# Grouped convolution by three products per image pair in place of four

## The reference, cut to what matters

```python
# x (32, 64, 1024), cond (32, 128), weight (64, 16, 9), c_weight (64, 128), bias (64,), kernel (1024, 1024) bool
out = lax.conv_general_dilated(x, weight, window_strides=(1,), padding=[(4, 4)],
                               dimension_numbers=('NCH', 'OIH', 'NCH'), feature_group_count=4)
ctx = jnp.einsum('nd,od->no', cond, c_weight)
out = out + ctx[:, :, None] + bias[None, :, None]
w = kernel * 2.0 - 1.0
y = scale * jnp.einsum('bsi,if->bsf', out, w)
return x + y
```

## Time and profile before

| | us |
|---|---|
| three runs | 180.5, 180.7, 181.5; median 180.7 |
| profiled execution | 180.59 |
| its span | 178.8 |
| TensorE busy | 171.2 (96%) |
| VectorE busy | 127.5 (71%) |
| ScalarE busy | 68.1 (38%) |
| GpSimd busy | 7.4 (4%) |
| granted TensorE clock, mean | 0.99 of full |

### The profile page before, as it was taken

One profiled execution on the slowest core, in us unless ns is written; L12 is line 12 of the kernel. 1 busy time (PEld: TensorE's weight loads), 2 busy tenths in 40 slices (PEclk: granted clock), 3 DMA queues, 4 the chain that ended last, 5 costly groups with the idle time before them and its releaser, 6 DMA issues.

```text
span 178.8 us, 2874 instructions
## 1 busy us (share of the span) xinstructions
PE 171.2 (96%) x1010; PEld 147.5 (83%) x1010; DVE 127.5 (71%) x188; ACT 68.1 (38%) x77; POOL 7.4 (4%) x18
## 2 busy tenths in 40 slices
PE   7699999999999999999999999999999999998991
PEld 2379888898989889988989898988998898986781
DVE  5736466979996877687675967596766877587662
ACT  3203993566452543329071634237061502042000
POOL 4230600000000000000000000000000000000000
PEclk9969999999999999999999999999999999999999
DMA  5589697768886792776757793778463650005006
GB/s 216 132 152 279 206 262 188 186 105 207 192 283 164 104 343 47 109 167 125 283 84 175 116 318 56 130 146 204 192 96 55 90 233 0 2 0 235 4 0 235
DMA packets 23629, 27.35 MB, mean 153 GB/s; under 512 B 2752, under 2 KB 19072, under 8 KB 23616
## 3 DMA queue, kind: packets, MB, share of 16 engines
q1 hardware_dynamic: 22176, 25.63, 56.8%
q0 software_dynamic: 368, 1.07, 2.4%
q10 hardware_dynamic: 1072, 0.48, 1.3%
HBM read 10.32 MB, written 8.40 MB: 105 GB/s over the span
## 4 chain that ended last, share of the span: by engine, by line
PE 93%; DMA 2%; DVE 1%; ACTq 1%; issue 0%; DVEq 0%
PE ps_conv L658 33%; PE ps_A L681 28%; PE ps_C L681 14%; PE ps_B L681 7%; DMA taps_nat<-weight 2%; PE ps_B L698 2%; PE ps_A L698 2%; PE ps_toep L698 2%; PE ps_C L698 2%; PE ps_toep L681 1%; PE ps_toep L636 1%; PE ps_C L647 1%; DVE sums L214 1%; PE ps_A L624 1%; DVE x_nat L513 0%
## 5 line engine op out<-in xcount | busy, mean ns | idle before, releaser
L658 PEld LDWEIGHTS ps_conv<-toeplitz,x_blk 128*128 128x128 f32 x512 | 60.4, 194 | 2.6 <-issue 0.8
L658 PE MATMUL ps_conv<-toeplitz,x_blk 128*128 128x128 f32 x512 | 60.8, 278 | 0.0
L475 DVE TENSOR_TENSOR y_sum<-ps_conv,shift 128x512 f32<-128x512 f32 (+1 forms) x33 | 22.2, 674 | 17.4 <-PE ps_conv L658 12.4
L373 ACT CAST hi_S<-sums 128x512 fp32r<-128x512 f32 x28 | 16.6, 620 | 43.4 <-DVE sums L492 42.7
L373 ACT CAST hi_A<-y_sum 128x512 fp32r<-128x512 f32 x24 | 14.0, 616 | 41.5 <-DVE y_sum L475 41.5
L358 ACT COPY x_phase<-x_nat 128x1032 f32<-128x1032 f32 x13 | 28.3, 2177 | 3.0 <-DMA x_nat<-x 3.0
L513 DVE SCALAR_TENSOR_TENSOR x_nat<-ps_A,scale_col,x_nat 128x512 f32<-128x512 f32 x27 | 20.3, 750 | 11.2 <-PE ps_A L681 11.2
L502 DVE TENSOR_TENSOR lo_S<-sums,hi_S 128x512 fp32r<-128x512 f32 x28 | 19.0, 680 | 0.0
L502 DVE TENSOR_TENSOR lo_A<-y_sum,hi_A 128x512 fp32r<-128x512 f32 x24 | 16.3, 682 | 1.7 <-ACT hi_A L373 1.7
L681 PE MATMUL ps_A<-sign_T,hi_S 128*128 128x512 f32 x56 | 16.2, 412 | 1.1 <-DVE x_nat L513 0.9
L681 PE MATMUL ps_A<-sign_T,lo_S 128*128 128x512 f32 x56 | 15.0, 389 | 0.0
(11 more groups left out here) (104 smaller groups left out, 174.3 us busy)
## 6 DMA issues: line engine op xcount, KB each, us to landing
x_nat<-x SPq DMA_DIRECT2D x16, 512.0 KB, 4.2
out<-x_nat SPq DMA_DIRECT2D x15, 512.0 KB, 4.8
x_blk<-x_phase SPq DMA_DIRECT2D x118, 64.5 KB, 2.5
w_bytes<-w_bool SPq DMA_DIRECT2D x2, 512.0 KB, 6.3
shift<-shift_dram POOLq DMA_DIRECT2D x1, 768.0 KB, 6.1
x_blk<-x_phase ACTq DMA_DIRECT2D x6, 64.5 KB, 3.7
x_blk<-x_phase POOLq DMA_DIRECT2D x4, 64.5 KB, 3.0
out<-x_nat SPq DMA_DIRECT2D x1, 256.0 KB, 2.9
```

Source lines behind the costliest of these rows:

```text
L373: nc.scalar.copy(hi[k][:, :, :], flat(operand(k))).then_inc(hi_ok[k], 1)
L475: nc.vector.tensor_tensor(y_sum[r][:, u, a, :].rearrange("m u a o -> m a u o"), ps_conv[:, a, u, :], shift_of(d, r, a).unsqueeze(2).to_bro ...
L658: now = nc.tensor.matmul(ps_conv[:, a].rearrange("m u o -> m (u o)"), x_blk[r][:, a, s:s + M], toeplitz[:, s, g].rearrange("r u o -> r u ( ...
```

## The change

*Three products.* Let the output rows m be even or odd. With x phases e = 0, 1, 2 (columns 2k, 2k+1, 2k+2), T0 and T1 the two halves of the Toeplitz form, the even output is x0 T0 + x1 T1 and the odd output x1 T0 + x2 T1. The changed kernel computes M1 = (x0 - x1) T0, M2 = x1 (T0 + T1) and M3 = (x1 - x2) T1; even = M1 + M2, odd = M2 - M3. x_phase holds the three in turn at a step of three floats (K = 64 columns each): GpSimd writes the two differences by one subtraction with 1024 results (differences), ScalarE copies the odd phases, 512 (odd_phases). Both images of the pair give one weight load of 128 columns at a step of 12 bytes, so one pair has 3 x 4 matmuls of 128 columns, in three banks of ps_conv, that of the middle product first. Blocks are 192 columns a phase in place of 129. Double 0 keeps four products; its phase copies have 1536 columns in place of 1032.

*Shift.* In doubles 1 to 7 one fp32r matmul of 512 columns over 64 rows puts the shift into the middle bank, from its high and low parts (shift_parts) and a 0/1 matrix (of_image) that GpSimd makes in two copies of 2048 columns on 32 rows each. The way through DRAM goes. The early matmul has 256 columns in place of 512.

*From banks to y.* ScalarE copies the middle bank (middle), VectorE adds and subtracts (y_of), giving y_two with (image, k) on the partitions. Four DMAs a pair of 128 KB each, issued by ScalarE (to_parity), carry it to y_sum with (parity, k) on the partitions. The rows of w_bool are loaded in that order too, by four DMAs in place of two.

*Parts and order.* High and low parts are made for two operands at once: A (A11 and A12), S12, S34, and A22 alone. S1 to S4 move from the end of step d - 1 to the start of step d. The convolution of pair (1, 0) follows plain product 5 in place of 4. x_nat keeps 11 pairs in place of 16, and a load waits for the store of the pair that it overwrites.

```diff
-EARLY = 8
+EARLY = 4
-CONV_AFTER = {4: 0, 6: 1}
+CONV_AFTER = {5: 0, 6: 1}
 ...
             def to_blocks(d, r):
-                sp.wait_ge(conv_done[r], 2 * d)
-                sp.wait_ge(phase_ok[r], B * (d + 1))
-                for a in range(NG):
-                    to_block(sp, r, a, blk_in[r][a // GROUPS])
+                if d == 1:
+                    sp.wait_ge(conv_0[r], 2)
+                else:
+                    for m in range(3):
+                        sp.wait_ge(m_done[m], order(d - 1, r) + 1)
+                sp.wait_ge(dif_ok[r], d)
+                sp.wait_ge(odd_ok[r], d)
+                for g in range(GROUPS):
+                    for i in range(2):
+                        a = i * GROUPS + g
+                        sp.dma_start(x_blk[r][:, 2 * g + i], x_phase[r][a * CG:(a + 1) * CG]).then_inc(blk_in[r], 16)
 ...
+            def differences(d, r):            # GpSimd
+                x_wait(pool, d, r)
+                first = line(d, r, 0, PAD + L + PAD)
+                left, right = (bass.AP(first.tensor, first[:, c:c + 1].offset, [first.ap[0], [1, B], [B, 2], [2 * B, K]])
+                               for c in (0, B))
+                nc.gpsimd.tensor_tensor(x_phase[r][:, :, :].rearrange("r q (k e) -> r q e k", e=3)[:, :, 0::2], left, right, ALU.subtract).then_inc(dif_ok[r], 1)
 ...
+            def odd_phases(d, r):             # ScalarE
+                x_wait(act, d, r)
+                nc.scalar.copy(x_phase[r][:, :, 1::3], line(d, r, B, B + L).rearrange("r (k p q) -> r q k p", p=2, q=B)[:, :, :, 0]
+                               ).then_inc(odd_ok[r], 1)
+            def middle(d, r):
+                act.wait_ge(m_done[1], order(d, r) + 1)
+                if d > 1:
+                    act.wait_ge(y_in[r], 16 * 4 * (d - 1))
+                nc.scalar.copy(y_two[r][:, 1].rearrange("m u (g o) -> m g u o", g=GROUPS), ps_conv[:, 1]).then_inc(mid_ok, 1)
+            def to_parity(d, r):
 ...
+                for p, made in ((0, y_even_ok), (1, y_odd_ok)):
+                    act.wait_ge(made, order(d, r) + 1)
+                    for i in range(2):
+                        act.dma_start(y_sum[r][p * K:(p + 1) * K, i], y_two[r][i * K:(i + 1) * K, p]).then_inc(y_in[r], 16)
 ...
             def step(d):                      # ScalarE
-                for k in ("S3", "S4", "A22"):
-                    high_part(k, d)
                 if runs(d, 4):
-                    to_phases(d + 2, 0)
+                    odd_phases(d + 2, 0)
+                high_part("S12", d)
                 if runs(d, 2):
-                    high_part("A12", d + 1)
-                    high_part("A11", d + 1)
+                    middle(d + 1, 0)
+                high_part("S34", d)
+                high_part("A22", d)
+                if runs(d, 2):
+                    to_parity(d + 1, 0)
+                    middle(d + 1, 1)
                 if runs(d, 4):
-                    to_phases(d + 2, 1)
+                    odd_phases(d + 2, 1)
                 if runs(d, 2):
-                    high_part("S1", d + 1)
-                    high_part("S2", d + 1)
+                    high_part("A", d + 1)
+                    to_parity(d + 1, 1)
             def first_double():
 ...
+                high_0("A11")
+                odd_phases(1, 0)
+                act.wait_ge(w_in[1], 32)
                 sign("B11", 1)
-                to_phases(1, 1)
+                odd_phases(1, 1)
                 sign("B12", 1)
+                high_0("A21")
+                middle(1, 0)
+                odd_phases(2, 0)
+                middle(1, 1)
+                to_parity(1, 0)
+                odd_phases(2, 1)
+                high_part("A", 1)
+                to_parity(1, 1)
 ...
+            def y_of(d, r):                   # VectorE
+                n = order(d, r)
+                even, uneven = (y_two[r][:, p].rearrange("m u (g o) -> m g u o", g=GROUPS) for p in range(2))
+                dve.wait_ge(mid_ok, n + 1)
+                dve.wait_ge(m_done[0], n + 1)
+                if d > 1:
+                    dve.wait_ge(y_in[r], 16 * 4 * (d - 1))
+                nc.vector.tensor_tensor(even, ps_conv[:, 0], uneven, ALU.add).then_inc(y_even_ok, 1)
+                dve.wait_ge(m_done[2], n + 1)
+                nc.vector.tensor_tensor(uneven, uneven, ps_conv[:, 2], ALU.subtract).then_inc(y_odd_ok, 1)
 ...
             def step(d):                      # VectorE, as it stands after
+                if d > 1:
+                    sum_up("C21_A", d - 1)
+                combine("S1", d)
+                combine("S2", d)
+                sum_up("C11_P2", d)
+                combine("S3", d)
+                combine("S4", d)
+                sum_up("C11_P1", d)
+                low_part("S12", d)
+                if runs(d, 2):
+                    y_of(d + 1, 0)
+                sum_up("C12_A", d)
+                low_part("S34", d)
+                sum_up("C22_C", d)
+                low_part("A22", d)
+                if runs(d, 2):
+                    y_of(d + 1, 1)
+                sum_up("C22_A", d)
+                if last(d):
+                    finish_last(d)
+                else:
+                    low_part("A", d + 1)
+                    sum_up("C12_C", d)
 ...
             def conv(d, r):                   # TensorE
+                n = order(d, r)
 ...
+                pe.wait_ge(blk_in[r], 16 * NG * d)
+                for m, taps, read in ((1, 2, mid_ok), (0, 0, y_even_ok), (2, 1, y_odd_ok)):
+                    if n:
+                        pe.wait_ge(read, n)
+                    if m == 1:
 ...
+                        nc.tensor.matmul(ps_conv[:, m], of_image[:, first:first + 2].rearrange("n i k -> n (i k)"),
+                                         shift_parts[:, :].rearrange("n (g o) -> n g o", g=GROUPS).unsqueeze(2)
+                                         .to_broadcast([2 * N, GROUPS, B, CG]), start=True, stop=False, skip_group_check=True)
                     for g in range(GROUPS):
+                        now = nc.tensor.matmul(ps_conv[:, m, g].rearrange("m u o -> m (u o)"),
+                                               x_blk[r][:, 2 * g:2 * g + 2].rearrange("r b n -> r (b n)")[:, m::3],
+                                               toeplitz[:, taps, g].rearrange("r u o -> r (u o)"), start=m != 1, stop=True,
+                                               skip_group_check=True)
+                    now.then_inc(m_done[m], 1)
```

More of the change, by code:

```diff
@@ L76, with conv_product_kernel @@
                 "C21_A": "P4"}
-def conv_product_kernel(nc, x, cond, bias, weight, c_weight, w_bool, scale, shift_dram, out):
+def conv_product_kernel(nc, x, cond, bias, weight, c_weight, w_bool, scale, out):
     x_pairs = x.rearrange("(j a) c l -> j (a c) l", a=2)
@@ L224, in signs_in, with group, parts, images @@
             rows = slice(half * KH, (half + 1) * KH)
-            eng.dma_start(w_bytes[:, rows, :], w_bool.rearrange("(m p) f -> m p f", p=B)[:, rows, :]).then_inc(w_in[half], 16)
+            for p in range(2):
+                eng.dma_start(w_bytes[p * K:(p + 1) * K, rows, :],
+                              w_bool.rearrange("(k p u) f -> p k u f", p=2, u=B)[p][:, rows, :]).then_inc(w_in[half], 16)
         def operand(k):
+            if k in s_sum:
+                return s_sum[k]
             half = slice(0, KH) if k in ("A11", "A21") else slice(KH, B)
-            return s_sum[k][:, :, :, :] if k in s_sum else y_sum[int(k[1]) - 1][:, half, :, :]
-        def flat(ap):
-            return ap.rearrange("m u a o -> m u (a o)")
+            return y_sum[int(k[1]) - 1][:, :, half, :].rearrange("m i u c -> m u i c")
+        def group(k):
+            if k == "A":
+                return y_sum[0][:, :, :, :].rearrange("m i u c -> m u i c")
+            if k in ("S12", "S34"):
+                n = 0 if k == "S12" else 2
+                return sums[:, n:n + 2].rearrange("m n u i c -> m (n u i c)")
+            return operand(k)
+        def parts(of, k):
+            n = OPERANDS.index(SPLITS[k][0])
+            both = of[:, n:n + len(SPLITS[k])]
+            if k in ("S12", "S34"):
+                return both.rearrange("m n u c -> m (n u c)")
+            return both.rearrange("m n u (i c) -> m (n u) i c", i=2)
+        def images(ap):
+            return ap.rearrange("m u (i c) -> m u i c", i=2)
         @block.sync
@@ L361, in high_part, with high_0 @@
+            def high_0(k):
+                act.wait_ge(y_0, 3 if k == "A12" else 4 * int(k[1]))
+                nc.scalar.copy(images(hi[k]), operand(k)).then_inc(hi_0[k], 1)
             def high_part(k, d):
-                if k in s_sum:
-                    act.wait_ge(s_ok[k], d)
-                elif d == 0 and k == "A12":
-                    act.wait_ge(y_ok, 3)
+                if k in ("S12", "S34"):
+                    for part in SPLITS[k]:
+                        act.wait_ge(s_ok[part], d)
@@ L367, in high_part @@
                 else:
```

(14 more changed lines are left out.)

366 lines of the change are left out of this document (182 added, 184 removed).

## The result

| | before | after |
|---|---|---|
| median of the runs, us | 180.99 (4 runs) | 224.76 (222.7 to 226.3, 4 runs) |
| span of the profiled execution | 178.8 | 223.0 |
| ratio | | 1.238 (95%: 1.228 to 1.248) |

Forecast was 178.8 us in a range of 175.0 to 188.5. The kernel became 24% slower. The medians are of all runs; ratios and, from here on, differences between two kernels leave out a run that took over 1.5% longer than the fastest of its kernel (224.3 us for after). The page of after has rows that answer to the earlier trace rows: the new convolution, its weight loads, and GpSimd with VectorE. Columns: busy us, mean ns of one, then the engine's idle time before them and its releaser.

A forecast was written before the change was run, and what follows sets the result against it. TensorE's own work was taken as the bound: 178.8 span + 5.3 for the first double - 7.0 for 11 later convolutions + 0.2 in the last step = 177.3, 179.1 with the 1.8; stated as 178.8, range 175.0 to 188.5.

The forecast's parts named there:

- TensorE's records: Convolution matmuls with weights at a 12-byte step: 0.109 us a record taken, 24 records in 2.61 us.
- the forecast's largest gain: Convolutions from the second double on: 2.84 us a pair against 3.48, 0.64 less, 9.0 us over 14 pairs.
- nothing waits for them: GpSimd's two subtractions a step, 3.6 us taken for each (2.2 to 4.4), claimed to delay nothing in the steady stretch.
- The lock: Rival: VectorE operations with two SBUF inputs and GpSimd's subtraction wait for each other; 188 taken, 186 to 196 and more; chance 0.15.
- my 4.9: Steady step: the second pair's subtraction starts when its load lands, 4.9 us into the next step.
- The transfers: Rival: DMA engines become the bound or y lands late; 188 at 20.2 us a step, 181 from landing alone; chance 0.15.
- The first double: Waits for blocks and y around the start of double 1 make its P6 5.3 us later than 48.92.
- the four times that I had forecast: Pair 2's blocks landed 31.2, pair 3's 37.4; in double 1, P2 starts at 45.4 and P6 at 54.2.
- my 50.0: First double: pair 3's y transfers, issued behind a high part until 47.5, land at 50.0.
- its 0.2: Last step: P6 waits for the C11 sum, whose low part now comes as one long piece, adding 0.2 us.
- Strided loads: Rival: convolution weight loads at a 12-byte step are slower; 190 at 1.3 times, 206 at 1.75 times; chance 0.06.
- the DMA load: Rival on transfers: DMA work of 16.7 to 25.2 us per 18.6 us step, 17.6 expected; chance 0.15.

The follow-up runs named there:

- e5: Kernel before, convolution weight columns read at steps of 1, 2, 3, 4, 6, 8, 5 floats by double; records 0.109, 0.116, 0.170, 0.227 us at steps 1 to 4.
- e6: Kernel before with useless GpSimd subtractions, copies and memsets between SBUF tiles added in doubles 2 to 5; 183.29 us (one run).
- e10: Changed kernel with packed weight columns, a memset for GpSimd's subtraction, the shift matmul on 128 rows, sign tiles ahead of x_nat; 192.62 us, 1.065.
- e12: As e10, but only two thirds of every later block transferred, with as many pieces and issues; 182.94 us, 1.004.
- e15: e11 with each block laid out in three pieces of 256 bytes per row, so weight loads are packed, everything computed; 206.24 us, 1.138.
- e11: Changed kernel, all computed: subtractions on VectorE, shift matmul on 128 rows, transfers of pair (1, 0) issued early; 202.68 us, 1.121.

## Why the prediction was wrong

**TensorE's records: the step that failed first.** "I take 0.109, because 12 bytes is much nearer to packed than 32." The bounds held (0.109 to 0.19), the choice did not: 0.175 in after, 0.170 in e5. The rows had no length for a strided weight load, and I interpolated along bytes between two points of another engine; the curve that e5 measured is nearly flat up to 8 bytes and from 16 on, and 12 lies half way up. It made the forecast's largest gain, 9.0 us, a loss: 14 x (4.64 - 3.48) = 16 us. I gave it a chance of 0.06 beside a page that spoke for it: the Trainium skill (Advanced Engine Details and Errata, SBUF Cachelines) asks for at least two hits on each 16-byte line. e5 agrees with it, reading 0.116 where a line has two hits (8 bytes), 0.170 where two lines of three have one, and 0.215 to 0.233 from there on, where each has one. An estimate from e5 that covers all four: 0.227 us times the 16-byte lines per element (a half, three quarters, one), and never under 0.109.

**GpSimd "nothing waits for them".** The subtraction took 4.57 us against the 3.6 that I took and 4.4 that I had as the end. The lock is the mechanism that I wrote as a rival at 0.15 and priced 186 to "196 and more". For the range I priced it at a subtraction of 2.6 us, though my own sum took 3.6; at 3.6 it stood outside the 188.5. e6 shows the lock by itself. In after, the second pair's subtraction starts 111.78 - 106.65 = 5.1 us behind P2, my 4.9, and holds the last S operation; the first pair's, which I had not placed in the step at all, holds the low part that P2 waits for. What I had held against it, a VectorE operation that stayed at 0.69 us beside GpSimd, was one with an input in PSUM; I said so, and then let it weigh all the same. The Trainium skill (SBUF, Who interferes with whom) states the lock as exclusive; the trace agrees, as a low part of 4.27 us ended 1.1 us after the subtraction, about its own length. The lock also reached into the sign tiles (L559, 4 x 2.4 us in the front), which I had not listed as reading SBUF twice.

**The transfers.** I summed 16.7 to 25.2 us of DMA work per 18.6 us step, expected 17.6, and took 2.5 us for a y landing. This rival too had 0.15. In the 25 us steps of after it hardly showed (VectorE's S operations waited 0.3 us for y in all), and it came out once the other two were gone: e10 to e12, 10.9 us for 32 KB less per block. The landing in the first double is where 2.5 is most wrong: in e10 pair 2's y arrives 4.9 us after its last issue, with 16 blocks and a load issued on the other queue in the 12 us up to then.

**The first double.** With light blocks (e12) the four times that I had forecast, 31.2, 37.4, 45.4 and 54.2, came out at 32.3, 37.4, 45.55 and 57.67. The order of waits was right; pair 3's y landed at 53.1, 3.1 us later than my 50.0. Not in my account: after 3 to 4 us of idle TensorE the granted clock fell (0.50 from 60.45 to 62.20 in e12), and groups of four took 1.7 us until it rose (58.76 to 60.45), some 2 us.

**The sum from P6 of double 1 to the end** was to be 123.1 us and was 155.5. By the terms: 11 convolutions x 1.6 = 17.6; the shift at 0.43 plus 0.1 for its gap, less 0.227, x 11 = 3.3; 384 product matmuls, 16 of them half as wide, x 0.0055 = 2.1; idle TensorE 155.5 - 146.2 = 9.3, of which the forecast held 4.7 (4.5 in before, and its 0.2), so 4.6; the lower clock behind the idle 5.57 us, some 2.0. That is 29.6 of 32.4, and 2.8 are not placed. In e12 it is 125.5, of which 2 are the low clock.

**Rivals.** Strided loads, the lock and the DMA load had 0.36 together, each as the only thing to go wrong. All three were true. Two of them stood side by side, one in TensorE's work and one in what TensorE waits for, so their prices did not add: 12.4 and 11.5 alone, 30.7 as a pair. The third hardly showed while the others were there; no run takes it alone out of after. No version beat the kernel before. The arithmetic of fewer products is sound (18.6 us a step), but only with weights that lie packed. Of the two ways tried, pieces of 256 bytes (e15) gained nothing over e11, and e12, which transfers a third too little and has no subtraction at all, only equals the kernel before. A smaller slip: seven low parts at 680 ns against three at 1214 and one at 680 is 0.4 us less for VectorE, not the 0.5 to 1 that I wrote; nothing hung on it.

**Open.** Why the place of the sign tiles in SBUF moves a matmul from 0.227 to 0.233 was not settled (neither 32 bytes nor the PSUM bank does it). Nor was a layout tried with two phases interleaved at a step of 8 bytes, two pieces in place of three. Nor is it shown how much of the 10.9 us of e12 comes from y's landing and how much from the blocks' (3.4 us in e10, 2.9 in e12).

## What to carry to other kernels

Price a strided weight load by measuring it before any saving in matmuls is counted: here a step of 12 bytes made a record 1.6 times as long, which is more than a quarter fewer records gives back. Before work is given to an idle GpSimd, list every VectorE instruction with both inputs in SBUF that can meet it; here each waited for the rest of GpSimd's subtraction. And when several rivals share one path, don't divide the chance between them as if one excluded the others: ask what is left when the first is removed, for that is also what a repair will run into.
